# The second layer norm's variance from the attention sum and its squares on ScalarE, the last pair's routing batch by batch, and the order of both ends written anew

## The reference, cut to what matters

```python
x = x + attention(layernorm(x))     # shell/charge features, causal 512x512 softmax, values, output weights
x = x + slots(layernorm(x))         # gelu, router over 64 slots, top 8 softmax, gather, GRU, scatter
def layernorm(x): m = mean(x); v = var(x); return (x - m) / sqrt(v + 1e-5)
```

## Time and profile before

| what | us |
|---|---|
| median of 3 runs | 690.5 |
| lowest and highest | 690.22, 690.83 |
| the profiled execution | 691.52 |
| its span, first to last instruction | 689.7 |
| granted TensorE clock, mean | 0.998 |

### The profile page before, as it was taken

The page is one execution under the profiler, slowest core; times in us unless marked ns, Lnnn a source line. Parts: engine busy times, 40 slices in busy tenths (PEclk is TensorE's granted clock), DMA queues, the critical chain, the costliest instruction groups (busy, mean ns, idle before and its releaser), DMA issues. The chain is left out here.

```text
span 689.7 us, 15834 instructions
## 1 busy us (share of the span) xinstructions
PE 670.2 (97%) x4622; PEld 540.4 (78%) x4622; DVE 605.0 (88%) x2001; ACT 513.7 (74%) x1477; POOL 384.9 (56%) x818
## 2 busy tenths in 40 slices
PE   8999999999899999999999999999999999999986
PEld 4877778787697887879798787879878787977764
DVE  6688898797989898998989899898989989898985
ACT  4879888867596896969688695968879596876451
POOL 3717767362665747376565737556583756655200
PEclk9999999999999999999999999999999999999999
DMA  8343020204233050323315032321404242121005
GB/s 229 116 153 91 2 63 1 63 2 137 47 96 89 10 162 16 122 63 110 75 35 150 2 126 60 123 63 57 129 2 138 49 123 62 63 62 63 1 2 182
DMA packets 49116, 54.11 MB, mean 78 GB/s; under 512 B 6213, under 2 KB 40583, under 8 KB 49031
## 3 DMA queue, kind: packets, MB, share of 16 engines
q1 hardware_dynamic: 48260, 52.57, 27.5%
q10 hardware_dynamic: 770, 0.53, 0.3%
HBM read 20.58 MB, written 16.78 MB: 54 GB/s over the span
## 5 line engine op out<-in xcount | busy, mean ns | idle before, releaser
L241 POOL TENSOR_TENSOR Z<-Z,QB 128x512 f32<-128x512 f32 x60 | 77.3, 1289 | 81.5 <-ACT Z L813 79.6
L758 ACT ACTIVATE xn<-X,rs 128x255 f32<-128x255 f32 x128 | 66.4, 600 | 72.4 <-POOL rs L1535 72.4
L443 PE MATMUL ps<-Vh,Eh 128*128 128x256 f32 x320 | 88.6, 304 | 0.1
L349 PE MATMUL ps<-W1h,xh 128*128 128x354 f32 x256 | 88.6, 346 | 0.1
L349 PE MATMUL ps<-W1h,xl 128*128 128x354 f32 x256 | 83.0, 324 | 0.6 <-DVE xl L1013 0.5
L349 PE MATMUL ps<-W1l,xh 128*128 128x354 f32 x256 | 82.9, 324 | 0.0
L443 PE MATMUL ps<-Vl,Eh 128*128 128x256 f32 x320 | 80.8, 280 | 0.0
L824 ACT ACTIVATE E<-ps,nmax 128x128 f32<-128x128 f32 (+3 forms) x128 | 67.8, 536 | 10.3 <-DVE nmax L1069 10.1
L1020 DVE TENSOR_TENSOR Vl<-ps,Vh 128x256 fp32r<-128x256 f32 x128 | 53.6, 421 | 22.9 <-ACT Vh L783 20.7
L1077 DVE TENSOR_TENSOR El<-ps,Eh 128x128 fp32r<-128x128 f32 (+3 forms) x128 | 61.7, 484 | 12.7 <-ACT Eh L834 11.2
L268 POOL TENSOR_SCALAR xm<-X,rs 128x256 f32<-128x256 f32 x120 | 67.7, 578 | 2.2 <-POOL rs L1544 1.0
...
## 6 DMA issues: line engine op xcount, KB each, us to landing
...
out_x<-X SPq DMA_DIRECT2D x4, 256.0 KB, 2.5
...
X<-in_W_v ACTq DMA_DIRECT2D x1, 256.0 KB, 4.5
X<-in_W_outT ACTq DMA_DIRECT2D x1, 256.0 KB
```

Source lines behind the costliest of these rows:

```text
L241: e.tensor_tensor(Z[:, i + 1, :], Z[:, i, :], QB[:, :], ALU.mult).then_inc(s["zm"], 1)
L349: ins = e.matmul(p[:, 0:FEATS], x[:, d, c, t * 128:t * 128 + 128], w[:, c, :], start=j == 0, stop=j == 5)
L443: ins = e.matmul(p[:, 0:D], w[:, r % 2, j * 128:j * 128 + 128], v[:, (2 * k + d) % 4, j, :], start=z == 0, stop=z == len(parts) - 1)
L758: ins = e.activation(xn[:, d, t, 0:D - 1], X[:, b % NX, t, 0:D - 1], ACT.Identity, bias=rs[:, d, 2, t:t + 1], scale=rs[:, d, 1, t:t + 1])
```

## The change

The second norm's statistics are computed otherwise. `attended` also writes the sum of its 256 results (accum_out) into `sums`. A new ACT step `lm_square` then computes Square(-256 x + sum) over the tile, with the sum as a per-row bias, and accumulates it, which gives 65536 times the sum of squared deviations. `lm_stats` is gone from DVE; `lm_variance_ops` is two small instructions instead of six, the first of which waits for `attended` alone. `attended` of a batch's first tile has a new wait for `lm_v` of the batch two before, and every `lm_square` waits for the one before it.

GI and GIN no longer have tiles of their own but lie in gn and gt, so `gi_copy` and `gathered` have a new wait for the new slots of the pair before.

For the last pair `route`, `rt_out` and `rt_t` are done for each batch by itself (`end_route`, `end_rt_out`, `end_rt_t`), and the last `gather` does the four tiles of the first batch and then those of the second.

The written-out order of PE, ACT, DVE and POOL is new in prologue and tail, and partly so in the loop. The diff, cut to its core:

```diff
-        stats2 = sb("stats2", [128, 2, 4, 6])
-        mv2 = sb("mv2", [128, 2, 4, 2])
+        sums = sb("sums", [128, 2, 2, 4])
+        squares = sb("squares", [128, D])
...
-        GIN = sb("GIN", [128, D])
-        GI = sb("GI", [128, 2, 2, S])
...
+        GI = gn
+        GIN = gt[:, :, :, :].rearrange("p c b s -> p (c b s)")
...
         def lm_variance_ops(e, k, d):
             b = 2 * k + d
+            e.wait_ge(s["av"], 8 * k + 7 + d)
+            e.tensor_scalar(rs2[:, d, 2, :], sums[:, d, 0, :], -1.0 / D, None, ALU.mult).then_inc(s["lm_m"], 1)
             e.wait_ge(s["lm_s"], 8 * k + 7 + d)
-            e.tensor_tensor(mv2[:, d, :, :], stats2[:, d, :, 1:3], stats2[:, d, :, 4:6],
-                            ALU.add).then_inc(s["lm_a"], 1)
-            e.wait_ge(s["lm_a"], b + 1)
-            e.tensor_scalar(rs2[:, d, 2, :], mv2[:, d, :, 0], -0.5, None, ALU.mult).then_inc(s["lm_m"], 1)
-            e.tensor_scalar(rs2[:, d, 1, :], mv2[:, d, :, 1], 1.0 / D, 1e-5, ALU.mult, ALU.add).then_inc(s["lm_e"], 1)
-
-            e.wait_ge(s["lm_m"], b + 1)
-            e.tensor_tensor(rs2[:, d, 0, :], stats2[:, d, :, 1], rs2[:, d, 2, :], ALU.add).then_inc(s["lm_d"], 1)
-            e.wait_ge(s["lm_d"], b + 1)
-            e.tensor_tensor(rs2[:, d, 0, :], rs2[:, d, 0, :], rs2[:, d, 0, :], ALU.mult).then_inc(s["lm_q"], 1)
-            e.wait_ge(s["lm_q"], b + 1)
-            e.wait_ge(s["lm_e"], b + 1)
-            e.tensor_tensor(rs2[:, d, 0, :], rs2[:, d, 0, :], rs2[:, d, 1, :], ALU.add).then_inc(s["lm_v"], 1)
+            e.tensor_scalar(rs2[:, d, 0, :], sums[:, d, 1, :], 1.0 / (D * 65536.0), 1e-5, ALU.mult, ALU.add).then_inc(s["lm_v"], 1)
...
+            def end_route(d):
+                p, before = G.take(s["rtT"], NP + d)
+                at["rt", NP - 1, d] = p
+                if before:
+                    e.wait_ge(*before)
+                e.wait_ge(s["h"], B - 1 + d)
+                e.matmul(p[own(d), :], w2[:, :], hT[:, d, :], start=True, stop=True).then_inc(s["rt_mm"], 1)
...
+            def end_rt_t(d):
+                p, before = T.take(s["dm"], B - 1 + d)
+                at["rtt", NP - 1, d] = p
+                if before:
+                    e.wait_ge(*before)
+                e.wait_ge(s["rtT"], NP + d)
+                for t in range(4):
+                    ins = e.transpose(p[:, t * S:t * S + S], RT[own(d), t * 128:t * 128 + 128], ident[own(d), own(d)])
+                ins.then_inc(s["rt_t"], 1)
...
-                for t in range(4):
-                    for d in range(2):
-                        if t == 0:
-                            e.wait_ge(s["am"], 2 * k + d + 1)
-                        ins = e.matmul(p[own(d), 0:D + 1], AL[:, t, d, :],
-                                       xm[:, (2 * k + d) % 3, t, 0:D + 1], start=t == 0, stop=t == 3)
+                turns = [(t, d) for t in range(4) for d in range(2)]
+                if k == NP - 1:
+                    turns.sort(key=lambda x: x[1])
+                for t, d in turns:
+                    if t == 0:
+                        e.wait_ge(s["am"], 2 * k + d + 1)
+                    ins = e.matmul(p[own(d), 0:D + 1], AL[:, t, d, :],
+                                   xm[:, (2 * k + d) % 3, t, 0:D + 1], start=t == 0, stop=t == 3)
...
-                proj(p, 0, 2); e_t(n, 1); gx_n(m); xn_t(p, 1, 1); values(n, 0); proj(p, 0, 3); logits(n, 1)
-                out_mm(g, 1); xm_t(f, 0, 0); xm_t(f, 0, 1); e_t(n, 2); proj(p, 1, 0); proj(p, 1, 1)
-                proj(p, 1, 2); proj(p, 1, 3); values(n, 1); xm_t(f, 1, 0); hidden(f, 0); xm_t(f, 1, 1)
-                values(n, 2); e_t(n, 3); e_t(n, 4); hidden(f, 1); q_t(p); logits(n, 2); route(f); e_t(n, 5)
+                proj(p, 0, 2); gx_n(m); xn_t(p, 1, 1); e_t(n, 1); values(n, 0); proj(p, 0, 3); xm_t(f, 0, 0)
+                logits(n, 1); out_mm(g, 1); e_t(n, 2); proj(p, 1, 0); xm_t(f, 0, 1); proj(p, 1, 1)
+                proj(p, 1, 2); proj(p, 1, 3); xm_t(f, 1, 0); values(n, 1); hidden(f, 0); xm_t(f, 1, 1)
+                e_t(n, 3); values(n, 2); e_t(n, 4); hidden(f, 1); q_t(p); logits(n, 2); route(f); e_t(n, 5)
...
-            out_mm(13, 0); gi_t(14); gx_rz(14); xm_t(15, 0, 0); xm_t(15, 0, 1); xm_t(15, 1, 0); gx_n(14)
-            xm_t(15, 1, 1); hidden(15, 0); hidden(15, 1); route(15); al_t(14); rt_t(15); slot_v(14); warm(12)
-            out_mm(13, 1); gather(15); out_mm(14, 0); gi_t(15); al_t(15); end_gx_r(); end_gx_nz()
...
+            values(15, 7); gather(14); out_mm(13, 0); gi_t(14); xm_t(15, 0, 0); xm_t(15, 0, 1); xm_t(15, 1, 0)
+            gx_rz(14); xm_t(15, 1, 1); hidden(15, 0); hidden(15, 1); end_route(0); gx_n(14); end_rt_t(0)
+            end_route(1); out_mm(13, 1); end_rt_t(1); warm(12); al_t(14); slot_v(14); gather(15)
+            out_mm(14, 0); gi_t(15); al_t(15); end_gx_r(); end_gx_nz(); out_mm(14, 1); residual(); slot_v(15)
+            out_mm(15, 0); out_mm(15, 1)
 
...
                 e.activation(xmT[:, d, c, :].bitcast(FR), at["xm", b, c][:, :], ACT.Copy).then_inc(s["xmT"], 1)
 
             @live
+            def lm_square(k, n):
+                r = 8 * k + n
+                b, t = 2 * k + n % 2, n // 2
+                e.wait_ge(s["av"], r + 1)
+                if r:
+                    e.wait_ge(s["lm_s"], r)
+                e.activation(squares[:, :], X[:, b % NX, t, :], ACT.Square, bias=sums[:, b % 2, 0, t:t + 1], scale=-256.0,
+                             accum_out=sums[:, b % 2, 1, t:t + 1]).then_inc(s["lm_s"], 1)
+
+            @live
             def gelu(k, d):
                 b = 2 * k + d
                 e.wait_ge(s["h_mm"], b + 1)
...
+            def end_rt_out(d):
+                e.wait_ge(s["rt_mm"], NP + d)
+                e.activation(RT[own(d), :], at["rt", NP - 1, d][own(d), :], ACT.Identity,
+                             bias=b2[own(d), 0:1]).then_inc(s["rtT"], 1)
...
+                    e.wait_ge(s["sn"], k)
...
+                lm_square(f, 3); lm_square(f, 4); lm_square(f, 5); lm_square(f, 6); ln_norm(p, 0); gi_copy(m)
+                xn_high(p, 0, 0); expo(n, 0); xn_high(p, 0, 1); ln_norm(p, 1); v_high(p, 0, 0); expo(n, 1)
+                expo(n, 2); xn_high(p, 1, 0); v_high(p, 0, 1); probs_t(n, 0); v_high(p, 0, 2); lm_square(f, 7)
+                rz_tanh(m); expo(n, 3); xn_high(p, 1, 1); probs_t(n, 1); v_high(p, 0, 3); xm_copy(f, 0, 0)
+                lm_square(n, 0); n_tanh(m); expo(n, 4); probs_t(n, 2); v_high(p, 1, 0); xm_copy(f, 0, 1)
+                v_high(p, 1, 1); expo(n, 5); v_high(p, 1, 2); v_high(p, 1, 3); xm_copy(f, 1, 0); gelu(f, 0)
+                xm_copy(f, 1, 1); probs_t(n, 3); charge(p); probs_t(n, 4); gelu(f, 1); sine(p); rt_out(f)
+                q_copy(p); probs_t(n, 5); z_copy(p); expo(n, 6); expo(n, 7); route_exp(f, 0); probs_t(n, 6)
...
+            lm_square(15, 4); lm_square(15, 5); lm_square(15, 6); lm_square(15, 7); al_copy(13); gi_copy(14)
+            xm_copy(15, 0, 0); xm_copy(15, 0, 1); xm_copy(15, 1, 0); xm_copy(15, 1, 1); gelu(15, 0)
+            rz_tanh(14); gelu(15, 1); end_rt_out(0); n_tanh(14); end_rt_out(1); route_exp(15, 0)
+            route_exp(15, 1); al_copy(14); gi_copy(15); end_r_tanh(); end_nz_tanh(); al_copy(15); last_copy()
...
+                    if b >= 2:
+                        e.wait_ge(s["lm_v"], b - 1)
                 e.scalar_tensor_tensor(X[:, b % NX, i, :], at["av", r][:, 0:D], rinv[:, r % 8:r % 8 + 1],
-                                       X[:, b % NX, i, :], ALU.mult, ALU.add).then_inc(s["av"], 1)
-
-            @live
-            def lm_stats(k, n):
-                r = 8 * k + n
-                b, t = 2 * k + n % 2, n // 2
-                d = b % 2
-                e.wait_ge(s["av"], r + 1)
-                if t == 0 and b >= 2:
-                    e.wait_ge(s["lm_d"], b - 1)
-                e.bn_stats(stats2[:, d, t, :], X[:, b % NX, t, :]).then_inc(s["lm_s"], 1)
+                                       X[:, b % NX, i, :], ALU.mult, ALU.add,
+                                       accum_out=sums[:, b % 2, 0, i:i + 1]).then_inc(s["av"], 1)
 
...
+                if k == NP - 1:
+                    return at["rtt", k, d][:, 0:4 * S].rearrange("p (t s) -> p t s", t=4)
...
+                e.wait_ge(s["rt_t"], k + 1 + (d if k == NP - 1 else 0))
...
+                    e.wait_ge(s["sn"], k)
+                e.tensor_scalar(GIN, p[:, 0:D], rw[:, 1:2], None, ALU.mult).then_inc(s["gin"], 1)
...
+                row_max(n, 5); inverse(n, 1); finish(g, 1, 1); v_low(p, 1, 0); v_low(p, 1, 1); v_low(p, 1, 2)
+                xm_low(f, 0, 1); probs_low(n, 2); attended(n, 1); v_low(p, 1, 3); xm_low(f, 1, 0)
+                xm_low(f, 1, 1); turns(p); new_slots(m); probs_low(n, 3); remainder(p); inverse(n, 2)
+                mirror(p); attended(n, 2); quarter_turn(p); probs_low(n, 4); row_max(n, 6); row_max(n, 7)
+                attended(n, 3); probs_low(n, 5); top(f, 0, 0); top(f, 0, 1); top(f, 1, 0); top(f, 1, 1)
```

(11 more changed lines are left out.)

388 lines of the change are left out of this document (179 added, 209 removed).

## The result

The changed kernel takes 692.56 us (median of 20 executions) beside 690.79 us of the kernel before (20): a ratio of 1.0024, with a 95% interval of 1.0015 to 1.0033. It is slower by just over the 0.2% that this measurement can tell, where 684.8 had been forecast. The 20 executions fall into two groups by their mean granted clock: twelve at 0.991 to 0.996 have a median of 693.61 (one of these twelve took 690.5), eight at 0.999 or 1.0 one of 691.05. The profiled execution (692.67, span 690.4) belongs to the first.

What follows compares the result with a forecast made beforehand. The prediction took PE to bound the loop, with DVE and ACT off the path. Gains of 2.2, 1.5, 0.8 and 1.2 us sum to 5.7, taking the median from 690.5 to 684.8 us, range 679.5 to 692.5.

Steps and rivals of the forecast that it cites:

- The loop's 2.2 us: Loop: shorter small PE waits were to save 0.2 us in each of eleven iterations, 2.2 us in all.
- two gaps in the queue of the weight loads: Loop: recurring PE weight-load waits of 0.15 and 0.25 us, of which at most 0.40 an iteration was to be gained.
- nothing gained: Whole kernel: waits only change names and the tail's gain is eaten; 690.0 us, chance 0.15.
- POOL's part: Loop: POOL does four small instructions fewer for each batch, and nobody on the path waits for that.
- a new wait that recurs in the loop: Loop: the sign named as what would make the forecast wrong, since it counts eleven times.
- Prices on ACT and DVE: Loop, each iteration: ACT gains 4.8 us for eight Squares; DVE loses 3.3 for statistics and gains 0.3 for sums.
- ACT becomes the bound: Loop: Squares make ACT late and PE stalls; 694 us, chance 0.13.
- The table rival: Squares between Gelu or Sin and the next Exp need additional table loads; 687.8 us, chance 0.07.
- The prologue: Ahead of the loop: 1.5 us gained in the 28.41 us stretch near its end, bounds 0 to 2.98.
- The wait for slot values: Prologue: PE's 1.51 us wait before slot values was to fall under 0.5.
- the zero: Prologue's first 155 us: no gain or loss, between +1 and -1 us.
- The tail: Behind the loop: 0.8 us gained up to the last norm, 1.2 us behind it, 0 in the last 18.40 us.

Runs made afterwards that it cites:

- e2: Changed kernel with POOL's loop order put back as before (power ahead of shift8, alpha ahead of the last power): 689.77 us, ratio 0.9987.
- e3: Changed kernel with both swaps undone, values_setup ahead of scale_a_setup on DVE and POOL's loop order: 687.76 us, ratio 0.9964.
- e1: Changed kernel with only the DVE start swap undone, scale_a_setup ahead of values_setup again: 691.04 us, ratio 1.0002.
- e7: Changed kernel with both swaps undone, and each Square on ACT cut to one column of the tile: 687.53 us, ratio 0.9957.
- e5: Kernel before the change with only the statistics moved to sums and ACT Squares, orders otherwise old, no routing by batch: 707.09 us, ratio 1.0250.
- e9: Kernel before with the statistics alone moved, plus POOL's first-batch norm ahead of the second batch's scale in the loop: 703.59 us, ratio 1.0192.
- e4: Kernel before the change with only the DVE start swap made, values_setup ahead of scale_a_setup: 690.84 us, ratio 1.0010.
- e17: Kernel before the change with only POOL's loop order taken from the changed kernel: 696.83 us, ratio 1.0096.
- e8: Changed kernel with both swaps undone, and the last gather's matmuls alternating between the two batches as before: 688.07 us, ratio 0.9971.
- e14: Changed kernel with both swaps undone, and the last pair's routing done for both batches together again: 692.55 us, ratio 1.0037.
- e11: Changed kernel with both swaps undone, eight warming matmuls instead of six, and a finish moved from between DVE's last tops: 692.05 us, ratio 1.0017.

## Why the prediction was wrong, point by point

Set against the profiled execution, the forecast span was 684.0 and the measured one 690.4. The 6.4 us lie in the loop (439.22, forecast 435.25: 4.0), ahead of it (184.24, forecast 182.08: 2.2) and in the tail (66.95, forecast 66.7: 0.25).

**The loop's 2.2 us were never there.** The step that failed: I read two gaps in the queue of the weight loads as time that PE loses. In e2, where DVE has its statistics off, the second still stands, in the same place of the iteration and with the same size:

```profile
376.53 0.19 PEld L433 LDWEIGHTS ps<-Vh,Eh 128*128 128x128 f32 x1 [0.26 <-DVE X L1132]
```

and the loop is 437.61. Of the nine loops without POOL's swap the shortest is 437.15, 0.3 below before's. Weight loads run beside matmuls (359.71 us of the one and 437.35 of the other in 437.45), and matmul time went on through these gaps; the row of PE, 0.1 us idle of 437.45, had said so, and I set a fine row against it. My rival "nothing gained" had the right loop.

**The loop's loss of 1.8 us.** The second step that failed, a term put at nothing: I priced POOL's part as four small instructions fewer, for which nobody on the path waits, and wrote that SP's queue is moved past by nothing. I did not read on in POOL's list, which is in the diff, though the earlier trace rows has the 5.85 us in which ACT waits for POOL. `shift8` ahead of `power` is a wait for DVE's top in front of work that is ready. The price is read from e2 and e3: 1.6 us of loop against the changed kernel and 2.5 against e1 (440.06), 2.8 and 3.3 of the median. I closed with "a new wait that recurs in the loop" as what would make me wrong; it was this one, and I had not looked for it in the one list that was in the diff and that I called harmless.

**Prices on ACT and DVE.** Forecast were 4.8 and -3.0 us for an iteration. ACT rose by (385.11 - 343.05) / 11 = 3.8, to 88%; DVE fell by (400.65 - 372.06) / 11 = 2.6, to 85%. For DVE that is inside the bounds, for ACT just under the lower one of 4.0: the Square took 520 ns and its read 208, a little more than the row that I had taken for each, but the read runs beside the end of the Square and the next instruction (in the changed profile a Square starts at 354.93, its read at 355.33, the next step at 355.43). The read of `attended`'s sum is 81 ns and hides beside the next instruction too. These terms were right enough, and beside the point.

**The rival "ACT becomes the bound"** did not occur in the changed kernel (e7). But in e5 a Square that comes late holds POOL, and POOL holds PE: its mechanism exists, by place in the queue; e9 shows that for 4.3 us, and for the rest of e5's loop it is open.

**The table rival** is out: the loads are 16, 17 and 18 where the earlier trace rows had 16, 19 and 18, two fewer and none more. The Trainium skill's statement (ScalarE: Activation LUTs, "Table sets: the hidden batching unit") that cheap functions stand in every set agrees with that, though it does not name Square among its examples.

**The prologue** was put at -1.5 us with 0 for its first 155, "between +1 and -1". The wait for slot values went from 1.51 to 0.77, so not under 0.5 as I had said it would. The stretch that this term was for, gather 1 to gather 2, was 28.41 in the kernel before, in e4 and in e17, and is 27.38 to 27.42 in every version with the new orders and the Squares: 1.0 of the 1.5 came. What failed is the zero, the third step. I had seen `values_setup` ahead of the first variance and gave it no price, because I asked only how long it runs and not for which load it waits. The fall of the clock behind it was a thing that no row of before showed, and my bound did not reach it: gather 1 came at 156.85. Without that swap it comes at 153.64 to 156.06 in the profiles of e1, e3, e7, e8 and e14, and with the start of before at 155.17, 153.53 (e4) and 154.06 (e17); up to there the new order neither gained nor lost more than these differ among themselves. e3 has new waits near 50 us (0.62, 0.89 and 0.58 in its profile), and there too the clock was once 0.86 and 0.80 in 50 to 60 us. These terms add up: 1.0 here and 1.9 in the tail make 2.9, and at full clock e3 is at 687.20 and the kernel before at 690.04.

**The tail** was right. Forecast were 0.8 up to the last norm and 1.2 behind it, 2.0 in all; measured 66.95 against 68.67, 1.7. The last norm began 31.7 us behind the gather of pair 13 (655.15), against 34.8 before (655.79): 3.1 earlier, forecast 3.0. That the sum fits so well is in part luck, for its sizes were off in two places that cancel: sorting the last gather is free (e8; it lasts 3.00, not 3.7), but alpha of batch 31 is ready at 672.26, 48.8 us behind gather 13, against 50.5 before: 1.7 earlier, where 2.9 was forecast (2.1, and the 0.8 ahead of it). New slots and a `finish` now stand between DVE's tops. Moving that `finish` to where e11 has it costs more than it gives.

**The range** of 679.5 to 692.5 missed 692.56 by a hair. The slower case that came was not the one that I had priced: no engine was too full, two queues had a wait in the wrong place. Undoing both gives 4.8 us of the 7.8 between forecast and median; the rest is for the most part the loop's 2.2 that could not be had, and the 0.5 missing in the prologue.
